# Causal mask of two of four batches as extra rows of the query and key stacks

## The reference, cut to what matters

```python
q, k = _apply_rotary(q, cos, sin), _apply_rotary(k, cos, sin)
attn = jnp.einsum('bhqd,bhkd->bhqk', q, k) * scale
causal = jnp.triu(jnp.ones((s, s), dtype=bool), k=1)
attn = jnp.where(causal, -jnp.inf, attn)
attn = jax.nn.softmax(attn, axis=-1)
...
x = x + attn_ref(layernorm(x))
x = x + xattn_ref(layernorm(x), ctx_1024)
x = x + ffn_ref(layernorm(x))
```

## Time and profile before

| what | us |
|---|---|
| median of 3 runs (180.1, 181.15, 181.98) | 181.15 |
| the profiled execution's own time | 179.57 |
| its span in the profile | 177.8 |
| TensorE busy (1548 products) | 163.0 |
| VectorE busy (448 instructions) | 127.2 |
| ScalarE busy (218) | 104.7 |
| GpSimd busy (132) | 68.1 |

### The profile page before, as it was taken

How to read it: one execution, slowest core, us unless ns; L and a number is a source line. 1 busy time by engine, 2 the same in 40 slices (tenths; PEclk the granted TensorE clock), 3 DMA queues, 4 the chain that set the end, 5 groups by cost and what they waited for, 6 DMA issues and landing times.

```text
span 177.8 us, 4415 instructions
## 1 busy us (share of the span) xinstructions
PE 163.0 (92%) x1548; PEld 117.6 (66%) x1548; DVE 127.2 (72%) x448; ACT 104.7 (59%) x218; POOL 68.1 (38%) x132
## 2 busy tenths in 40 slices
PE   5798996999998899899899899899999998989993
PEld 4467874767675667476577557557675565979983
DVE  4487578985988988899989969999965355551200
ACT  2056522276666566566577767866756766971351
POOL 6708969298704442060160250210341071224230
PEclk9999999999999999999999999999999999999999
DMA  5923264474374164163063064005304402617300
GB/s 153 297 42 113 87 158 114 114 177 116 90 173 143 45 161 116 37 155 87 4 169 100 2 153 108 9 7 163 105 9 140 126 4 66 200 30 208 94 30 30
DMA packets 23449, 18.39 MB, mean 103 GB/s; under 512 B 2428, under 2 KB 21372, under 8 KB 22780
## 3 DMA queue, kind: packets, MB, share of 16 engines
q1 hardware_dynamic: 22672, 17.20, 36.4%
q10 hardware_dynamic: 756, 0.92, 1.9%
HBM read 12.08 MB, written 2.29 MB: 81 GB/s over the span
## 4 chain that ended last, share of the span: by engine, by line
PE 60%; DVE 24%; POOL 4%; issue 4%; DMA 3%; ACT 2%; SPq 0%; POOLq 0%; DVEq 0%; ACTq 0%
PE psV L993 12%; DVE negmax L673 10%; PE psA L942 9%; PE psB L971 9%; PE psA L1037 6%; PE psV L1054 4%; DVE xn L626 3%; PE psM L853 3%; PE psA L1054 3%; DVE stats L617 2%; POOL rstd L524 2%; PE psB L976 2%; PE psB L1037 2%; PE psB L876 2%; DMA stackQ<-maxT 2%
## 5 line engine op out<-in xcount | busy, mean ns | idle before, releaser
L807 ACT ACTIVATE E<-psB 128x512 f32<-128x512 f32 x112 | 62.2, 595 | 23.9 <-PE psB L976 13.5
L673 DVE TENSOR_REDUCE negmax<-psA 128x2 f32<-128x512 f32 (+1 forms) x76 | 48.1, 681 | 8.3 <-PE psA L942 4.2
L942 PE MATMUL psA<-stackK,stackQ 72*128 72x256 bf16 (+1 forms) x256 | 41.8, 259 | 2.3 <-DVE negmax L673 2.3
L971 PE MATMUL psB<-stackQ,stackK 74*128 74x256 bf16 (+1 forms) x256 | 41.2, 259 | 0.6 <-DMA stackQ<-maxT 0.2
L993 PE MATMUL psV<-E,V 128*18 128x256 f32 (+1 forms) x512 | 30.5, 356 | 0.0
L942 PEld LDWEIGHTS psA<-stackK,stackQ 72*128 72x128 bf16 x256 | 21.8, 98 | 12.3 <-DVE negmax L673 5.2
L667 DVE CUSTOM_DVE_ANT_0 masked<-psA,row_mask 128x128 bf16<-128x128 f32 (+1 forms) x96 | 27.8, 349 | 3.0 <-PE psA L942 3.0
L971 PEld LDWEIGHTS psB<-stackQ,stackK 74*128 74x128 bf16 x256 | 21.9, 97 | 7.4 <-ACT E L807 3.1
L523 POOL TENSOR_SCALAR rstd<-mv 128x2 f32<-128x2 f32 x12 | 2.7, 229 | 56.9 <-DVE mv L621 56.9
L993 PEld LDWEIGHTS psV<-E,V 128*18 128x18 f32 x512 | 11.8, 97 | 13.0 <-issue 6.5
L976 PE MATMUL psB<-mask16T,ident 128*128 128x256 bf16 (+1 forms) x48 | 14.8, 309 | 0.0
(11 more groups left out here) (114 smaller groups left out, 249.3 us busy)
## 6 DMA issues: line engine op xcount, KB each, us to landing
stackK<-scratch SPq DMA_DIRECT2D x18, 192.0 KB
stackQ<-hid SPq DMA_DIRECT2D x36, 64.0 KB
w1s<-w_dram SPq DMA_DIRECT2D x8, 258.0 KB, 2.8
w2s<-w_dram SPq DMA_DIRECT2D x8, 256.0 KB, 3.8
stackQ<-scratch SPq DMA_DIRECT2D x2, 576.0 KB
stackK<-hid SPq DMA_DIRECT2D x16, 64.0 KB
scratch<-parts_ctx SPq DMA_DIRECT2D x12, 64.0 KB
stackQ<-scratch ACTq DMA_DIRECT2D x1, 576.0 KB
```

What stands on the lines that cost most here:

```text
L673: dve.tensor_reduce(negmax[:, b, heads[0]:heads[-1] + 1:2, t], scores[:, :, 0:keys], AX_X, ALU.max, negate=True).then_inc(a_taken, 1)
L807: act.activation(dst, psB[:, bank].rearrange("p (h q) -> p h q", h=dst.shape[1]), ACT.Exp, scale=SCALE).then_inc(b_taken, 1)
L942: last = pe.matmul(psA[:, bank, i * keys:(i + 1) * keys], stackQ[0:ROWS, b, h, t * P:(t + 1) * P], stackK[0:ROWS, b, h, 0:keys], start=(no ...
L971: last = pe.matmul(psB[:, bank, i * n:(i + 1) * n], stackK[:, b, h, t * P:(t + 1) * P], stackQ[:, b, h, q0:S], start=(s == 1 or i == 0), s ...
```

## The change

Batches 2 and 3 (the third and fourth) get their mask in the scores' own product. The stacks grow from 74 to 120 rows (CAUSAL = ROWS + KEPT). Rows 72 and 73 stay the max rows. Rows 74 on hold a staircase of steps of three positions: row 74 + m belongs to positions 3m to 3m + 2 of a block of 128, m from 0 to 42. In stackK such a row is 0 up to its first position, then 2^-51, then 1, and 2^51 from the fourth on; in stackQ it is 0 except at its own three positions, with -2^76, -2^25 and -2^-26. Each query meets one nonzero row, and the product with a key behind it is -2^25 or less, with a key before it at most 2^-26 in size. So the diagonal blocks are computed over 120 rows, the others over 72 (maxima) or 74 (exponentials), and a product of 256 columns that has both kinds becomes two of 128. The mask products L976 of these batches go, and their maxima are taken as in batch 0, with one reduction per unit, without a mask.

What is added: a step "stairs" in the start list, in which GpSimd builds the two staircases in E[0:48, 1] with two memsets, seven selects and a memset; two steps "stack_keep", each of two DMAs on SP that copy the staircases to rows 72 to 119 of a batch's stackQ and stackK, for all 16 heads; waits for these on TensorE (before the first maxima of the batch) and on ScalarE (before group 1 writes E[:, 1]). The ones for rows 72 and 73 of stackK are copied by L419 for batches 0 and 1 alone.

The diff:

```diff
--- before.py
+++ after.py
@@ -49,6 +49,10 @@
 ROWS = NPART * BLOCK
 NFILL = NPART * NPART
 MAXROW = ROWS
+KEPT = 48
+CAUSAL = ROWS + KEPT
+STEP = 3
+FIRST_KEPT = 2
 VW = 32
 VC = HD + 1
 NPAIR = NG // 2
@@ -60,6 +64,9 @@
 WARM = 16
 MASKED = -2.0 ** 100
 LARGEST = 2.0 ** 126
+KEY_TOP = 2.0 ** 51
+KEY_STEPS = ((3, 1.0), (2, 2.0 ** -51), (1, 0.0))
+QUERY_STEPS = ((3, -2.0 ** -26), (2, -2.0 ** 25), (1, -2.0 ** 76), (0, 0.0))
 
 FFN_STEPS = ((-11, "u0"), (-10, "u1"), (-9, "u2"), (-8, "u3"), (-4, "u4"), (-3, "u5"), (-1, "u6"), (1, "u7 g0"),
              (2, "d0 g1 g2"), (3, "d1 d2 g3"), (4, "d3 g4 g5"), (5, "d4 s0 g6 g7"), (7, "u8 d5"), (8, "d6 u9 d7 d8"),
@@ -80,13 +87,13 @@
         extra.setdefault(half, []).append(step)
 
     start = [("keep_warm", 0, 0), ("ln_stats", 0, 0), ("constants", 0, 0), ("ln_apply", 0, 0), ("ln_turn", 0, 0),
-             ("ln_stats", 0, 1), ("ln_apply", 0, 1), ("qk_self", 0, 0), ("ln_turn", 0, 1),
+             ("ln_stats", 0, 1), ("stairs", 0, 0), ("ln_apply", 0, 1), ("qk_self", 0, 0), ("ln_turn", 0, 1),
              ("ctx_turn", 1, 0), ("ctx_turn", 1, 1), ("qk_cast", 0, 0), ("ln_stats", 0, 2), ("qk_self", 0, 1),
              ("ln_apply", 0, 2), ("ln_stats", 0, 3), ("stack_fill", 0, 0)]
     start += [("q_select", 0, 0, g, u) for g in range(2) for u in range(2)]
     start += [("ln_turn", 0, 2)]
     start += [("q_select", 0, 0, g, u) for g in range(2, NG) for u in range(2)]
-    start += [("stack_put", 0, 1), ("stack_fill", 0, 1), ("constants", 0, 1)]
+    start += [("stack_put", 0, 1), ("stack_keep", 0, 3), ("stack_fill", 0, 1), ("stack_keep", 0, 2), ("constants", 0, 1)]
     put(1, "v_self", 0, 0)
     put(2, "qk_self", 0, 2)
     put(2, "stack_get", 0, 1)
@@ -275,8 +282,8 @@
         parts = hid[:, 0:3].rearrange("p n c t -> p (n c t)").bitcast(BF16).rearrange(
             "p (b w i t) -> p b w i t", b=NB, w=2, i=NPART)
         parts_ctx = sb("parts_ctx", [P, NB, NPART, S], BF16)
-        stackQ = sb("stackQ", [MAXROW + 2, NB, NH, S], BF16)
-        stackK = sb("stackK", [MAXROW + 2, NB, NH, S], BF16)
+        stackQ = sb("stackQ", [CAUSAL, NB, NH, S], BF16)
+        stackK = sb("stackK", [CAUSAL, NB, NH, S], BF16)
         ones16 = sb("ones16", [P, S], BF16)
         V = sb("V", [P, 2, NB, NT, NH // 2, 3 * VC])
 
@@ -291,6 +298,7 @@
         E = sb("E", [P, 3, GH, NT, S])
         one_hot = E[:, 2].rearrange("p h t s -> p (h t s)").bitcast(BF16)[:, 0:NH * 5 * BLOCK].rearrange(
             "p (h c) -> p h c", h=NH)
+        kept_k, kept_q = (E[0:KEPT, 1, h, 0].bitcast(BF16)[:, 0:S].rearrange("r (n q) -> r n q", n=NT) for h in range(2))
         oT = sb("oT", [P, 2, NPAIR, S])
         rden = sb("rden", [P, 2, NT * NH])
         oN = sb("oN", [P, 2, NT, D])
@@ -337,6 +345,7 @@
         gate_in, bproj_in = sem("gate_in"), sem("bproj_in")
         ident_set, row_mask_set, consts, v_init, v_zeroed = sem("ident_set"), sem("row_mask_set"), sem("consts"), sem("v_init"), sem("v_zeroed")
         ones16_set, ones_in = sem("ones16_set"), sem("ones_in")
+        kept_set, kept_in = sem("kept_set"), sems("kept_in", NB - FIRST_KEPT)
         misc_full, misc_taken = sems("misc_full", 2), sems("misc_taken", 2)
         var_ready, rstd_ready, xn_ready = sem("var_ready"), sem("rstd_ready"), sem("xn_ready")
         parts_k_self, parts_q_self = sems("parts_k_self"), sems("parts_q_self")
@@ -415,9 +424,9 @@
 
             sp.wait_ge(ones16_set, 1)
             for i in range(2):
-                half = ones16[i * P // 2:(i + 1) * P // 2, :]
-                sp.dma_start(stackK[MAXROW + i:MAXROW + i + 1].rearrange("o b h t -> o (b h) t"),
-                             half).then_inc(ones_in, 16)
+                part = FIRST_KEPT * NH
+                sp.dma_start(stackK[MAXROW + i:MAXROW + i + 1, 0:FIRST_KEPT].rearrange("o b h t -> o (b h) t"),
+                             ones16[i * part:(i + 1) * part, :]).then_inc(ones_in, 16)
 
             for st in steps:
                 kind, s, b = st["kind"], st["s"], st["b"]
@@ -429,6 +438,11 @@
                     for i in range(NPART):
                         for r in range(NPART):
                             fill_q(b, i, r, parts_q[b])
+                if kind == "stack_keep":
+                    for stack, kept in ((stackQ, kept_q), (stackK, kept_k)):
+                        sp.wait_ge(kept_set, len(KEY_STEPS) + len(QUERY_STEPS) + 1)
+                        src = kept[:, :, :].rearrange("r n q -> r (n q)").rearrange("r (o q) -> r o q", o=1)
+                        sp.dma_start(stack[ROWS:CAUSAL, b], src.to_broadcast([KEPT, NH, S])).then_inc(kept_in[b - FIRST_KEPT], 16)
                 if kind == "stack_write":
                     if st["g"] == 1:
                         write_k(s, b, parts[:, b, 1], parts_k_self[b])
@@ -488,6 +502,8 @@
                 ins.then_inc(pool_own, 1)
                 pool.wait_ge(pool_own, own[0])
 
+            made = [0]
+
             def split(src, dst, ready):
 
                 pool.tensor_copy(dst[:, 0], src).then_inc(ready, 1)
@@ -516,6 +532,15 @@
             pool.memset(ident16[:, :], 0.0)
             then(pool.memset(row_mask[:, :], 0.0))
             then(pool.memset(mask16[:, :, :], 0.0))
+
+            def stairs(rows, steps):
+
+                for least, below in steps:
+                    pool.affine_select(out=rows[:, :, :], in_=rows[:, :, :], compare_op=ALU.is_ge, fill=below,
+                                       base=2 * STEP - least, pattern=[[0, NT], [1, P]],
+                                       channel_multiplier=-STEP).then_inc(kept_set, 1)
+                    made[0] += 1
+                    pool.wait_ge(kept_set, made[0])
 
             def rsqrt_var(n, b):
 
@@ -539,6 +564,13 @@
                     causal(mask16, 1)
                     pool.wait_ge(consts, 4)
                     pool.tensor_copy(row_mask[:, P:S], mask16[:, 0, :]).then_inc(row_mask_set, 1)
+                if kind == "stairs":
+                    pool.wait_ge(rope_first, 1)
+                    then(pool.memset(kept_k[:, :, :], KEY_TOP))
+                    then(pool.memset(kept_q[:, :, :], 0.0))
+                    stairs(kept_k, KEY_STEPS)
+                    stairs(kept_q, QUERY_STEPS)
+                    pool.memset(kept_k[0:2], 1.0).then_inc(kept_set, 1)
                 if kind == "constants" and b == 1:
                     pool.memset(v_pairs[:, :, VC:2 * VC], 0.0).then_inc(v_init, 1)
                     then(pool.memset(mask16T[:, :, :], 0.0))
@@ -658,7 +690,7 @@
                     nh = len(heads)
                     scores = psA[:, bank].rearrange("p (h k) -> p h k", h=nh)
                     keys = (t + 1) * P if s == 0 else S
-                    if s == 0 and b > 0:
+                    if s == 0 and 0 < b < FIRST_KEPT:
                         if g == 0 and u == 0:
                             dve.wait_ge(row_mask_set, 1)
                         if unit >= 2:
@@ -795,6 +827,9 @@
                 if kind == "scores_exp":
                     grp = job * NG + g
                     u, bank = st["u"], unit % 2
+                    if grp == 1 and u == 0:
+                        for done in kept_in:
+                            act.wait_ge(done, 32)
                     if grp >= 3 and u == 0:
                         act.wait_ge(v_full, grp - 2)
                     act.wait_ge(b_full, unit + 1)
@@ -928,6 +963,8 @@
                     if unit == 0:
                         pe.wait_ge(consts, 4)
                     if g == 0 and u == 0:
+                        if s == 0 and b >= FIRST_KEPT:
+                            pe.wait_ge(kept_in[b - FIRST_KEPT], 32)
                         if job > 0:
                             pe.wait_ge(q_in[b], own_q(b) + 16 * NFILL * s)
                         pe.wait_ge(k_in[b], own_k(b) + 16 * NPART * s)
@@ -938,10 +975,15 @@
                     heads, t = unit_of(s, g, u)
                     keys = (t + 1) * P if s == 0 else S
                     by_product = s == 0 and b == 0
+                    spans = [(0, keys, ROWS)]
+                    if s == 0 and b >= FIRST_KEPT:
+                        spans = [(k, P, CAUSAL if k == t * P else ROWS) for k in range(0, keys, P)]
                     for i, h in enumerate(heads):
-                        last = pe.matmul(psA[:, bank, i * keys:(i + 1) * keys], stackQ[0:ROWS, b, h, t * P:(t + 1) * P],
-                                         stackK[0:ROWS, b, h, 0:keys], start=(not by_product or i == 0),
-                                         stop=not by_product, skip_group_check=True)
+                        for k, n, rows in spans:
+                            last = pe.matmul(psA[:, bank, i * keys + k:i * keys + k + n],
+                                             stackQ[0:rows, b, h, t * P:(t + 1) * P], stackK[0:rows, b, h, k:k + n],
+                                             start=(not by_product or i == 0), stop=not by_product,
+                                             skip_group_check=True)
```

(14 more changed lines are left out.)

## The result

The changed kernel took 182.91 us in the median of 22 runs, the kernel before 181.70 us in 22 runs beside it: a ratio of 1.0107, 95% interval 1.0075 to 1.0138. It is slower by 1.1%. Ratios here take in the fast runs alone (those over 1.5% above the fastest of their kernel, one of 395.8 us among them, are left out), so they aren't quotients of the medians. The forecast was 179.9 us with a range up to 182.6; the time lies outside it and on the other side. The profiled execution took 181.2 us, its span is 179.3 us (177.8 before).

The account below looks back on a forecast made before the run. TensorE was taken to set the pace from 44 to about 90 us, VectorE close behind, and a serial chain the start. Saving 3.3 us and spending 1.8 + 0.2 gave 1.3 us less: 179.9 us, range 177.3 to 182.6.

Parts of the forecast that it names:

- TensorE and VectorE, the sizes: Scores of batches 2 and 3: dropped mask products save TensorE 3.52 us, plain reductions save VectorE 3.0 us.
- What of this reaches the end: From 43.8 to 99.5 us, removed masks and waits shorten the kernel by 3.3 us, bounds 1.6 and 5.0.
- By window: Savings in four windows: 43.8 to 56.3 us nothing, to 70.8 us 2.0, to 85.6 us 1.0, to 99.5 us 0.3.
- that of batch 3's maxima: Window 56.3 to 70.8 us: 1.1 us of masks and 0.9 us of waiting for xn go, 2.0 us together.
- The wait for xn: TensorE's 0.9 us wait for normalised rows in 56.3 to 70.8 us mostly goes, as VectorE is freer; 0.9 us saved.
- The start: GpSimd's staircase build delays batch 2's root and everything behind it: 1.8 us lost, bounds 0.8 and 4.6.
- The 0.3 us for VectorE's delay: At the start, GpSimd's selects and VectorE's subtractions disturb each other; 0.3 us was taken as the cost.
- the 1.9 us worked out for four subtractions: At the start, upper price if each of four VectorE subtractions costs one select's length, 4 x 0.48 us.
- Rival B: Start: GpSimd's selects and VectorE's subtractions block each other, start costs 4.6 us; 1.8 us slower, 182.9 us; chance 0.15.
- DMA: Four added staircase transfers on SP's queue use slack ahead of batch 0's max rows: 0.2 us, bounds 0 and 1.3.
- Rival D: Added transfers hold up the max rows of batch 0 by the full 1.3 us: 181.0 us; chance 0.04.
- Sum: Whole kernel: 3.3 us saved, 1.8 + 0.2 spent, so 1.3 us less.

Follow-up runs that it names:

- gain alone: Changed kernel's score form over 72 and 74 rows, no staircases built or transferred, causal mask of batches 2 and 3 left out; ratio 0.989 to the kernel before.
- Cost alone: Changed kernel that builds and transfers the staircases but keeps the old masks of batches 2 and 3; 185.21 us, ratio 1.027 to the kernel before.
- stairs alone: GpSimd builds the staircases as in the changed kernel, but nothing transfers or uses them, masks as before; ratio 1.0045 to the kernel before.
- numbers 6 and 7: 6: changed kernel, staircases in idle w2 buffer, batch 3's transfers behind its reads, ratio 1.034; 7: staircases for batch 3 alone, built at half step 10, ratio 1.019.
- number 2: Changed kernel plus twice eight unused products of 256 columns in TensorE's idle time around the turn to batch 1's maxima; 182.60 us, ratio 1.013.

## Why the prediction was wrong

**TensorE and VectorE, the sizes: right.** Products of 128 columns over 120 rows follow each other as those over 72 did, and the reductions took 0.68 us each.

**What of this reaches the end: 3.3 us forecast, 2.4 measured in the changed kernel, 2.0 (0.9 to 3.0) with the gain alone.** By window: 0 forecast, 0.1 lost; 2.0 forecast, 0.8 measured; 1.0 forecast, 1.5; 0.3 forecast, 0.2. The mis-sized term is that of batch 3's maxima (2.0 us). The wait for xn shrank only from 0.9 to 0.6 us, and I had not looked at what TensorE would be early for: the query fills, for which it now waits:

```profile
PE psA L983 <- DMA stackQ<-hid: 0.7, 1, 0.7
PE psM L888 <- DVE xn L658: 0.6, 1, 0.6
```

**The start: 1.8 us forecast, 1.3 measured.** GpSimd's chain was priced at 15.2 us and ended at 15.02. The 0.3 us for VectorE's delay were a mistake of adding. Two subtractions at 11.18 took 1.15 us together and two at 12.34 took 1.07, where each pair took 0.76 before. The rule of the Trainium skill (SBUF — State Buffer, "Who interferes with whom") agrees with the trace in that the two engines block each other, and each pair lost about the length of one select (0.40 us), 0.7 us in all and not the 1.9 us worked out for four subtractions. But GpSimd is late anyway and xn waits for it, so VectorE's delay lies beside and adds nothing. Rival B, which built on it, was wrong.

**DMA: 0.2 us forecast, up to 1.3; this step failed.** Cost alone less stairs alone is 2.2% or 4.0 us (some 2.6 to 5.4 by the intervals of the two); the profile of the changed kernel shows 2.7. Three things were wrong in it. First the price, by an estimate: 1.57 MB by the rate of the earlier trace rows divided by its share gave 5.5 us. In the windows above (15 to 26 and 26 to 36 us) the engines were busy 0.18 x 11 + 0.35 x 10 = 5.5 us longer, but for 39 x 11 + 60 x 10 KB, 1.03 MB, more: 187 GB/s, by which 1.57 MB take 8.4 us. (Other transfers moved in time between the windows, so this is rough.) Second, I looked at the slack of the two transfers next to the added ones in one queue (fills and max rows) and not at the chain of DMAs between: the write to DRAM, the read back, and the fills that share engines with them. Third, and most of it: I priced a DMA wait as its own length. Here TensorE's clock went down to 1.2 GHz behind 0.9 us of waiting, in a stretch in which it had much to do, and that cost 1.6 us more. That this wait alone lowered it is not shown, for the clock can fall without it (numbers 6 and 7); that longer idle time makes it fall in nearly every run is what the runs of both kernels and number 2 point to. Rival D named the right resource, but the wrong transfer and half of the price.

**Sum.** 1.3 at the start, 2.7 in batch 1's stretch, less 2.4 from there on: 1.6 us, and 1.5 us more in the spans of the profiles (179.3 against 177.8); the runs say 1.0107, 1.9 us with 1.4 to 2.5.

## What to carry to other kernels

Before adding transfers to a schedule that is full of them, count the engines' busy time in the windows where they must run and list everything with a deadline that shares the engines, in any queue: moving the transfers moved the wait in all seven kernels that tried it. Price a wait of TensorE with what its clock may do afterwards (1.4 to 1.6 us in the three profiles where it fell once near 33 us), and where it already idles for a microsecond, keep it from idling further. And when a stage gets shorter, look first for the serial chain that feeds the next one: part of what the masks had cost turned into a wait for nine query fills.
